# Seven block products in place of eight for one more third of a gated feed-forward layer, and one transfer moved to another queue

## What is computed

```python
def lora_add(base, inp, A, B):            # A, B: the adapter of each batch, rank 16
    t = einsum('bri,bni->bnr', A[ids], inp)
    return base + einsum('bor,bnr->bno', B[ids], t) * 0.5

gate = lora_add(einsum('bnh,fh->bnf', x, W_gate), x, A_gate, B_gate)    # 512 -> 1376
up   = lora_add(einsum('bnh,fh->bnf', x, W_up), x, A_up, B_up)          # 512 -> 1376
act  = silu(gate) * up
down = lora_add(einsum('bnf,hf->bnh', act, W_down), act, A_down, B_down)
x1   = x + down @ sign(weight).T + bias0
out  = x1 + (B then A of adapter itok_B_4_50 on x1) + x1 @ W1.T + lora + bias1
```

## Time and profile before

| | |
|---|---|
| median of 3 runs | 877.64 us (876.82 to 879.19) |
| the profiled execution, its own time | 876.61 us |
| its span, first to last instruction | 874.8 us |
| TensorE busy | 868.2 us (99%) |
| VectorE busy | 523.5 us (60%) |
| ScalarE busy | 230.8 us (26%) |
| GpSimd busy | 86.5 us (10%) |
| transfers | 197.22 MB, mean 225 GB/s |
| granted TensorE clock | 0.999 of full speed |

### The profile page before, as it was taken

The page is one execution under the profiler, slowest core; times in us unless marked ns, Lnnn a source line. Parts: engine busy times, 40 slices in busy tenths (PEclk is TensorE's granted clock), DMA queues, the critical chain, the costliest instruction groups (busy, mean ns, idle before and its releaser), DMA issues.

```text
span 874.8 us, 21938 instructions
## 1 busy us (share of the span) xinstructions
PE 868.2 (99%) x7474; PEld 714.5 (82%) x7474; DVE 523.5 (60%) x1204; ACT 230.8 (26%) x460; POOL 86.5 (10%) x122
## 2 busy tenths in 40 slices
PE   9999999999999999999999999999999999999998
PEld 6888888888888888888888888888888888888885
DVE  5797555656555565656556655655656565556644
ACT  4953221222222122222212222212123122212210
POOL 0232000000000000000000000000000000000011
PEclk9999999999999999999999999999999999999999
DMA  9957777575777767577776757677775757777653
GB/s 338 415 218 251 237 232 249 188 242 156 235 248 227 244 209 238 156 234 231 236 236 226 241 166 233 195 248 239 230 243 176 235 175 243 246 226 247 204 133 94
DMA packets 161819, 197.22 MB, mean 225 GB/s; under 512 B 58112, under 2 KB 127744, under 8 KB 154112
## 3 DMA queue, kind: packets, MB, share of 16 engines
q1 hardware_dynamic: 103584, 108.76, 40.4%
q10 hardware_dynamic: 56096, 80.76, 27.3%
q0 software_dynamic: 2112, 7.34, 2.1%
HBM read 150.37 MB, written 15.20 MB: 189 GB/s over the span
## 4 chain that ended last, share of the span: by engine, by line
PE 95%; SPq 2%; DMA 1%; DVE 1%; issue 0%; ACT 0%; ACTq 0%; DVEq 0%
PE gu_ps L1132 54%; PE y_ps L1237 26%; PE out_ps L1259 3%; PE gu_ps L1346 2%; PE out_ps L1310 2%; PE gu_ps L1337 1%; PE y_ps L1132 1%; PE out_ps L1246 1%; PE out_ps L1132 1%; PE gu_ps L1237 1%; PE out_ps L1267 1%; DMA rows_sb<-in_btab 1%; SPq L352 0%; SPq L444 0%; DMA la_raw<-in_la 0%
## 5 line engine op out<-in xcount | busy, mean ns | idle before, releaser
L1237 PE MATMUL y_ps<-down_sb,actT_sb 128*128 128x512 f32 x1023 | 246.9, 394 | 0.0
L1237 PEld LDWEIGHTS y_ps<-down_sb,actT_sb 128*128 128x128 f32 x1023 | 189.7, 188 | 58.7 <-issue 21.4
L1132 PE MATMUL gu_ps<-wg_sb,xT_sb 128*128 128x432 f32 x768 | 163.8, 362 | 0.5 <-DVE act_all L842 0.5
L1132 PE MATMUL gu_ps<-wu_sb,xT_sb 128*128 128x432 f32 x768 | 160.7, 358 | 0.0
L1132 PEld LDWEIGHTS gu_ps<-wg_sb,xT_sb 128*128 128x128 f32 x768 | 141.7, 188 | 11.6 <-DVE xT_sb L824 1.4
L1132 PEld LDWEIGHTS gu_ps<-wu_sb,xT_sb 128*128 128x128 f32 x768 | 144.4, 188 | 8.0
L544 POOL TENSOR_TENSOR b_two<-b_raw,const_sb 128x128 f32<-128x128 f32 x62 | 23.5, 400 | 630.2 <-DMA b_raw<-in_b1tab 630.2
L598 ACT CAST actT_sb<-landed 128x512 fp32r<-128x512 f32 (+1 forms) x96 | 50.5, 584 | 127.1 <-issue 76.7
L610 ACT ACTIVATE act_all<-gu_ps 128x432 f32<-128x432 f32 (+1 forms) x96 | 49.6, 551 | 88.6 <-PE gu_ps L1337 83.6
L1132 PE MATMUL gu_ps<-slot,s_sb 128*128 128x512 f32 x270 | 66.8, 392 | 0.0
L846 DVE STREAM_TRANSPOSE act_all<-act_all 128x512 f32<-128x512 f32 (+1 forms) x96 | 64.0, 667 | 3.3
(11 more groups left out here) (173 smaller groups left out, 911.6 us busy)
## 6 DMA issues: line engine op xcount, KB each, us to landing
slot<-t_table ACTq DMA_DIRECT2D x59, 1024.0 KB, 7.7
a_raw<-in_atab SPq DMA_DIRECT2D x128, 152.0 KB, 7.5
rows_sb<-in_btab SPq DMA_DIRECT2D x128, 118.0 KB
landed<-act_all SPq DMA_DIRECT2D x132, 64.0 KB, 2.5
xT_raw<-in_xT SPq DMA_DIRECT2D x32, 256.0 KB, 6.3
x_in<-in_x SPq DMA_DIRECT2D x32, 256.0 KB, 8.1
landed<-act_all ACTq DMA_DIRECT2D x124, 64.0 KB, 2.7
out_x<-out_sb SPq DMA_DIRECT2D x31, 256.0 KB, 5.2
```

Source lines behind the costliest of these rows:

```text
L1132: last = nc.tensor.matmul(o, w, m, start=start and n == 0, stop=stop and n == len(terms) - 1, skip_group_check=not check)
L1237: last = nc.tensor.matmul(to[:], actT_sb[:, ACTT_SLOT[c] + n, a, :], down_sb[:, blk, b, :], start=begin and (c, n) == (0, 0) and (a, b) == ...
```

## The change

The third chunk is made like the middle one from step 2 on. Its blocks are called `v11` to `v22`, its products `q1` to `q7`, its sums of weights `vt1` to `vt4`, and its sums of results `v2`, `v4`, `vup_even`, `vup_odd`, `vgate_odd`. `SEVEN_MM` and `SEVEN_SUM` are the orders in which products and sums are counted on the semaphores `seven_mm` and `seven_sum`. The sums of weights are stored whole in `vt_table` (432 KB each) and are split on the chip each time they are loaded (`high_side_t` on ScalarE, `low_side_t` on VectorE). The order of blocks on TensorE is new, `s4` is made of three operations and not of two, `first_sums` and the splits of `s1` and `s2` stand ahead of `add_out` and of silu, and behind odd steps SyncE sends chunk 1 of the activations too. The sends of `x1` by ScalarE behind an odd step stand in the next even step.

```diff
-MID_MM = ("p1", "p6", "p5", "p3", "p7", "p4")
-MID_SUM = ("u2", "u4", "up_even", "up_odd", "gate_odd")
-S_RAW = ("s1", "s2", "s3", "s4_part", "s4")
+SEVEN_MM = ("p1", "q1", "p5", "q5", "p6", "q6", "p3", "q3", "p7", "q7", "p4", "q4")
+SEVEN_SUM = ("u2", "u4", "v2", "v4", "up_even", "vup_even", "up_odd", "vup_odd", "gate_odd", "vgate_odd")
+S_RAW = ("s1", "s2", "s4_a", "s4_b", "s4", "s3")
...
                     load_sbd(sp, cond)
+                    if parity == 1:
+                        send_act(sp, g, 1)
                     send_act(sp, g, 2)
...
             load_b(table_rows(SP, 0, 0))
+            sp.dma_start(vt_raw[1][:], wside[:, half(0)]).then_inc(S["vraw_in"], 16)
+            sp.dma_start(vt_raw[3][:], wside[:, half(2)]).then_inc(S["vraw_in"], 16)
+            sp.dma_start(vt_raw[2][:], wside[:, half(3)]).then_inc(S["vraw_in"], 16)
+            sp.dma_start(vt_raw[4][:], wside[:, half(1)]).then_inc(S["vraw_in"], 16)
...
             pool.wait_ge(S["raw1_in"], 32)
-            pool.wait_ge(S["wu_lo"], KC - 1)
+            pool.wait_ge(S["block_lo"], 4)
             difference(t1_raw, t3_raw, t1_raw)
...
             t_store(1, S["first_out"])
+
+            def side_difference(o, a, b):
+                nc.gpsimd.tensor_tensor(vt_raw[o][:], vt_raw[a][:], vt_raw[b][:], ALU.subtract).then_inc(S["vt_raw"], 1)
+
+            pool.wait_ge(S["vraw_in"], 4 * 16)
+            side_difference(1, 3, 1)
...
+            for n in range(1, 5):
+                pool.dma_start(vt_table[n - 1], vt_raw[n][:].rearrange("p k w -> p (k w)")).then_inc(S["vt_out"], 16)
             t_store(2, S["first_out"])
...
+            def load_side_t(n):
+                at = (n - 1) % 2
+                act.dma_start(vslot_raw[at][:].rearrange("p k w -> p (k w)"), vt_table[n - 1]
+                              ).then_inc(L[("vslot0_in", "vslot1_in")[at]], 16)
+
+            def high_side_t(n, j):
+                at = (n - 1) % 2
+                act.wait_ge(L[("vslot0_in", "vslot1_in")[at]], 16 * (2 * j - (n < 3)))
+                copy(vslot_sb[at][:, 0, :, :], vslot_raw[at][:]).then_inc(L["vt_hi"], 1)
...
+            def odd_products(g, j, prev):
+                add_block("up_odd", j, gu_ps[1][:], u4_sb[:], gu_ps[0][:], "p7", nth(SEVEN_SUM, "u4", j))
+                add_block("vup_odd", j, gu_ps[3][:, 0:SIDE], v4_sb[:], gu_ps[2][:, 0:SIDE], "q7", nth(SEVEN_SUM, "v4", j))
+                add_block("gate_odd", j, gu_ps[0][:], u2_sb[:], gu_ps[0][:], "p4", None)
+                add_block("vgate_odd", j, gu_ps[2][:, 0:SIDE], v2_sb[:], gu_ps[2][:, 0:SIDE], "q4", None)
...
+            def odd_blocks(g, j):
                 pe.wait_ge(L["act_done"], g * NC - NC + 2)
                 pe.wait_ge(L["s_lo"], nth(S_SPLIT, "s3", j))
                 slot_ready(0, 2 * j)
-                mid(0, s_of(1), slot_sb[0], L["mid_mm"], True)
-
-            def p4(g, j):
-                pe.wait_ge(L["mid_sum"], nth(MID_SUM, "up_odd", j))
+                one(0, s_of(1), slot0, L["seven_mm"], True)
+                pe.wait_ge(L["act_done"], g * NC)
+                side_ready(3, j)
+                one(2, s_of(1), vslot0, L["seven_mm"], True, SIDE)
+                pe.wait_ge(L["xT_lo"], g + 1)
+                summed("up_odd", j)
                 slot_ready(1, 2 * j - 1)
-                mid(0, x_of(1), slot_sb[1], L["mid_mm"], False)
+                one(0, x_of(1), slot1, L["seven_mm"], False)
+                summed("vup_odd", j)
+                side_ready(4, j)
+                one(2, x_of(1), vslot1, L["seven_mm"], False, SIDE)
...
             def step(g, j, parity, prev, pp):
...
                 elif parity == 0:
+                    even_blocks(g, j)
                     small_ready(g, prev, pp)
                     small(parity, prev, pp)
+                    summed("u2", j)
+                    first_gate(g)
+                    summed("v2", j)
+                    first_up(g, L["xT_used"])
                 else:
+                    odd_blocks(g, j)
+                    first_gate(g)
                     small_ready(g, prev, pp)
                     small(parity, prev, pp)
-                gate(g, 2)
-                up(g, 2)
+                    first_up(g, L["xT_used"])
```

More of the change, by code:

```diff
@@ L462, in load_x @@
             def load_x(g):
[L463 to L465 removed]
+                sp.dma_start((x_last if last(g) else x_in)[:], x[bass.ds(g * P, P), :]).then_inc(L["x_in"], 16)
             def store(g):
@@ L689, in step @@
                     load_b1end(g)
-                for c in range(NC):
-                    silu(g, c)
-                send_act(act, g, 0)
-                if not last(g):
-                    send_act(act, g, 1)
-                else:
-                    load_c(act, table_rows(ON_ACT, 1, prev), range(2, GB))
                 if parity == 1 and nxt is not None:
@@ L699, in step @@
                     high_s(2, j + 1)
+                for c in range(NC):
+                    silu(g, c)
+                if parity == 1 and nxt is not None:
+                    high_side_t(1, j + 1)
+                    high_side_t(2, j + 1)
+                send_act(act, g, 0)
+                if last(g):
+                    load_c(act, table_rows(ON_ACT, 1, prev), range(2, GB))
+                elif parity == 0:
+                    send_act(act, g, 1)
                 if first(g):
@@ L1152, in up, with whole @@
-            def up(g, c):
-                w = CHUNKS[c][1]
-                if c == 0 and first(g):
-                    pe.wait_ge(S["wu_lo"], KC)
-                product(gu_ps[GU_BANK[c][1]][:, 0:w], side(xT_sb, wu_sb, slice(SIDE_AT[c], SIDE_AT[c] + w)),
-                        L["xT_used"] if c == 2 else None)
-            def mid(bank, x_parts, w, signal, start):
-                product(gu_ps[bank][:], [(x_parts(k, a), w[:, b, k, :]) for k in range(HALF) for a, b in THREE], signal,
+            def whole(o, halves, signal=None):
+                product(o, [(xT_sb[:, k, a, :], halves[k // HALF][:, b, k % HALF, :]) for k in range(KC) for a, b in THREE], signal)
@@ new lines, in first_chunk, with first_gate, first_up @@
+            def first_chunk(bank, w, signal=None):
+                product(gu_ps[bank][:, 0:FIRST], [(xT_sb[:, k, a, :], w[:, b, k, :]) for k in range(KC) for a, b in THREE], signal)
+            def first_gate(g):
+                if first(g):
+                    pe.wait_ge(S["wg_lo"], 2)
+                pe.wait_ge(L["xT_lo"], g + 1)
+                after(pe, L["act_done"], g * NC - NC + 1)
+                first_chunk(GU_BANK[0][0], wg_sb)
+            def first_up(g, signal):
+                if first(g):
+                    pe.wait_ge(S["wu_lo"], 2)
+                first_chunk(GU_BANK[0][1], wu_sb, signal)
@@ L1162, in mid, with one, x_of @@
+            def one(bank, x_parts, w, signal, start, width=MID):
+                product(gu_ps[bank][:, 0:width], [(x_parts(k, a), w[:, b, k, :]) for k in range(HALF) for a, b in THREE], signal,
                         start=start, check=False)
-            def x_of(half):
-                return lambda k, a: xT_sb[:, half * HALF + k, a, :]
+            def x_of(h):
+                return lambda k, a: xT_sb[:, h * HALF + k, a, :]
             def s_of(at):
```

388 lines of the change are left out of this document (225 added, 163 removed).

## The result

The changed kernel takes 892.08 us, the median of 4 runs (889.79 to 893.90), where the kernel before took 877.80 beside it: a ratio of 1.016, with a 95% interval of 1.013 to 1.019. It is 1.6% slower; the forecast was 870.5 us, and the range ended at 878.5. The profiled execution took 893.9 us, its span is 891.8.

The account below looks back on a forecast made before the run. It took TensorE, busy 868.2 of 874.8 us, as the bound. Terms of -17.6 + 4.5 + 6 = -7.1 us gave a median of 870.5 us, range 863.5 to 878.5.

Parts of the forecast that it names:

- Term 1, the product that goes: Third chunk on TensorE: 42 in place of 48 matmuls of 432 columns a pair, 17.6 us less over 15 pairs.
- Term 2, p4's wait: Start of odd steps: p4 waits for VectorE's sum up_odd, 0.3 us a pair, 4.5 us in all.
- Reading GpSimd's bias as harmless to `up_odd`: Odd steps: GpSimd's bias runs beside up_odd, which reads one input from PSUM, so nothing was counted.
- What lies beside ... I count nothing: Extra VectorE and ScalarE work and SyncE's sends in the loop: covered by TensorE, counted as no cost.
- Transfers ... I take it as met: Loop loads: 1.77 MB more a pair, share about 0.81; slot and side loads land in time, no cost.
- the third rival: Even step's load x_in lands late, VectorE holds up_odd, p4 waits 1.3 us a pair: 886 us; chance 0.12.
- Term 3, the opening: Opening: t2's store goes out behind the side products' stores and lands late, step 1 ends 6 us later.
- a wait of TensorE for a transfer in the loop: Listed sign that the forecast is wrong: TensorE waiting for a transfer inside the loop; no size given.

Follow-up runs that it names:

- run 11: Changed kernel with side loads issued late, the opening's stores interleaved with the differences, and x for odd steps loaded by ScalarE ahead of its burst; 866.90 us.
- run 3: Changed kernel with chunk 1 of the activations sent by ScalarE again behind odd steps; 901.10 us.
- run 6: Changed kernel with ScalarE's loads of the third and fourth side product issued later, behind its copies of the landed activations; x1's sends not moved; 881.50 us.
- run 4: Changed kernel with side-product loads cut to a quarter of their bytes, engine work kept the same; 879.18 us.
- run 5: Changed kernel with both halves of x1 sent early, by ScalarE and SyncE, only from odd into even steps; 881.42 us.
- run 7: Changed kernel with the opening's side stores interleaved with GpSimd's differences and t2 stored between the second and third difference; 884.57 us.
- run 9: Changed kernel with the transposed x for odd steps loaded by ScalarE ahead of its four loads, in place of by SyncE; 887.65 us.
- run 2: Changed kernel with both halves of x1 sent early, by ScalarE and, in all steps, by SyncE ahead of the adapter rows; 948.76 us.

## Why the prediction was wrong, step by step

- **Term 1, the product that goes** (-17.6): right. Even steps take 28.44 = 27.27 + 6 x 0.195 us, odd ones 20.88 = 23.17 - 2.34 + 0.05, and run 11 has nearly nothing else in its loop. The row's 0.195 us a matmul was the price to take. The Trainium skill ("TensorE: Matmul & The Clock Gate", section "Back-to-back issue gap") gives 182.5 ns for a lone matmul, by which an even step would take 28.37 us; the trace does not agree.
- **Term 2, p4's wait** (+4.5): the mechanism is there, the size was too large. It cost 0.05 us a pair, 0.7 us in all, where 4.5 were put down: the sum began at 1.82 us of the step in place of 1.95, and p4 followed 0.05 us behind its end, where I had put 0.2. Reading GpSimd's bias as harmless to `up_odd` was right (0.67 us with the bias beside it at 448.56), while `s_raw` with two inputs in SBUF took 1.52.
- **"What lies beside ... I count nothing"**: this step failed. Two parts of it stood there: VectorE's splits ahead of `add_y`, SyncE's extra sends. They were held against q5's and the rows' due times, but the item that they push is x1, and x1's send was not followed to the product that reads it. The third was not named: ScalarE's half of x1 now stands in the even step behind the copy of `s4` and a side load, and run 3 shows that this half alone is enough for the wait. Before, it was issued at 4.7 us of the even step and wanted at 11.7, 7 us for a landing of 2.9 at most. Now it is issued at 8.8 and wanted at 12.7, which leaves 4 us, enough for a landing of 2.2 to 2.9, and the new side loads around it make that up to 5.9. Neither half of it costs much alone: runs 6 and 4 have the late issue without the burst and lose 2.3 and 3.0 us, run 5 has the burst behind an early issue and loses 2.9, and 1.7 of each is step 6 behind step 5's stall. Together they cost 18.4 us: 14.3 are waits that the profile puts down to x1, and about 1.4 are the clock behind one of them (last section).
- **"Transfers ... I take it as met"**: it looked at when the new loads land, not at what they land in front of. And it placed only the two side loads of the odd step; the third rival says "in even steps the burst is as before", yet the loads for the third and fourth side product go out in the even step, at 7.8 and 10.0 us, and those are the two around x1. The share of 0.82 was forecast as 0.81, and it is harmless: run 11 carries 260 GB/s and does not wait. It also missed that the move of the first sums makes VectorE wait for x ahead of the gated products: 3.8 us in step 5.
- **Term 3, the opening** (+6): right in kind, too small: 10.5 us. t2 landed at 92 for 91, and the activations of step 0 landed beside the same burst (10.9 us from issue to landing for the longest, by the chain of waits), which the forecast did not price. Runs 7 and 11 gain 6.5 and 5.9 us of it by order alone. The 4 to 5 us that stay begin with the differences, as far as the trace tells, since no run takes the differences away: a split of x took VectorE 2.49 us beside them (0.69 in the loop), TensorE waited 2.83 us behind it, and its clock was at 0.93 between 60 and 110 us.
- **The end** was not in the forecast: of the 2.3 us that the last odd step should save 1.7 are lost again. Step 31 is 1.8 us shorter (22.45 for 24.21), and what follows it is 1.2 us longer: TensorE waits 1.52 and 0.89 us for VectorE's splits of the last activations, where it waited 0.88 before.
- The ledger: -17.6 + 0.7 + 10.5 + 18.4 + 3.8 + 1.7 = 17.5, less 0.7 for one odd step of 23.87 in the profile before: 16.8 of the 17.0 us.
- **The rivals.** The third, with a chance of 0.12, held the right side (slower) and the wrong transfer: it had `x_in` late in front of p4, at 886 us. Of the signs of being wrong, "a wait of TensorE for a transfer in the loop" is the one that came, and it had no rival and no chance of its own: one row for each send on which TensorE waits, with issue, landing and due time, would have asked the question.

## What to carry to other kernels

When a change adds loads and lengthens queues, list every transfer that TensorE waits for with three times: issued, landed, wanted; then ask for each what is newly issued shortly before it, on any queue. Small urgent transfers go ahead of large patient ones, and a large one that must land only in the next step is held back on purpose until they are gone. A send in several parts is as late as its last part. And an engine that is made to stand still for an urgent item pushes everything behind it: look what then overtakes.

## What the runs showed of the hardware

- Transfers of different queues hold each other up, and an early issue helps. A quarter of x1 (64 KB) lands in 2.0 to 2.4 us in run 6, and in up to 5.9 in the changed kernel, between two loads of 432 KB. The load of the transposed x (256 KB) lands in 2.6 to 3.3 us ahead of ScalarE's burst in odd steps (run 9), in 3.7 to 4.4 behind the start of one or two side loads but ahead of the slots (changed kernel), and in 6.1 to 8.5 when it goes out 1 us behind the start of the burst, within 0.2 us of the first 1 MB slot load or behind it (run 2). It is no strict order of issue: in step 8 two quarters left at 274.36 and 274.38, and landed after 3.2 and 5.9 us. The Trainium skill ("DMA: Bandwidth & Descriptors", section "Issuing engines are not separate DMA queues") says that transfers issued by different engines run on the same 16 DMA engines and interleave; the traces agree, and add the price for the late starter.
- TensorE's clock fell behind some of its waits, and their length alone does not tell which. In run 2 it waited 2.00 us before 271.50 and 3.59 us before 381.66; the next 4 us (clock third from the end):

```profile
271.50:275.50 4.00, 4.00 (x18) 3.49 (x19) 3.97 (x6) 1.03 (x2) 0.97 (x1) 1.00 0.80 233
381.66:385.66 4.00, 4.00 (x13) 3.53 (x14) 3.97 (x6) 0.58 (x1) 2.06 (x2) 0.66 0.57 158
```

  In the changed kernel it is the other way round, for the waits of 3.31 us before 214.31 and of 2.10 us before 280.52:

```profile
214.31:218.31 4.00, 4.00 (x18) 3.46 (x19) 3.97 (x6) 1.05 (x2) 0.76 (x2) 1.00 0.62 160
280.52:284.52 4.00, 4.00 (x98) 3.72 (x99) 1.65 (x9) 0.87 (x2) 0.00 (x0) 0.57 0.42 81
```

  A mean of 0.66 or 0.57 is part of the stretch at 1.2 GHz and part at 2.4. In run 2 the step behind the wait of 3.59 us took 30.15 us and the one behind 2.00 us took 28.57, so the lower clock costs 1.6 us. Step 8 of the changed kernel is 3.7 us longer than 28.44: `small` begins 2.3 us late, and the other 1.4 us are the clock. What decides when it falls stays open.
- GpSimd and VectorE. In the opening, splits of 864 columns with both inputs in SBUF took 2.65 us beside GpSimd's differences and 1.04 alone. The Trainium skill ("SBUF — State Buffer", section "SBUF: two separate sides") calls the port pair that the two share an exclusive lock; the durations agree with waiting for it.
